# Expert results weighted per slot and added in DRAM by accumulating scatters onto the layer's input plus half the attention stream

## The reference, cut to what matters

```python
x = x + 0.5 * ffn(layernorm(x))        # f = 0
x = x + rwkv(layernorm(x))
x = x + 0.5 * ffn(layernorm(x))        # f = 1

def ffn(h0):                           # 16 heads, 4 key/value heads, 8 experts, 2 per token
    h = h0 + attention(rmsnorm(h0))
    return h + moe(rmsnorm(h))

def moe(xt):
    topv, topi = top_k(xt @ gate_w, 2)
    w = one_hot(topi) weighted with softmax(topv)
    for e in range(8):
        out += w[:, e:e + 1] * ((silu(xt @ w1[e]) * (xt @ w3[e])) @ w2[e])
```

## Time and profile before

| | us |
|---|---|
| median of 3 runs | 1247.35 |
| lowest, highest | 1242.57, 1247.72 |
| profiled execution | 1246.85 |
| its span (first to last instruction) | 1245.0 |
| PE busy in the span | 1167.7 (94%) |
| DVE busy | 939.9 (75%) |
| ACT busy | 798.2 (64%) |
| POOL busy | 567.9 (46%) |

### The profile page before, as it was taken

How to read it: one execution, slowest core, us unless ns; L and a number is a source line. 1 busy time by engine, 2 the same in 40 slices (tenths; PEclk the granted TensorE clock), 3 DMA queues, 4 the chain that set the end, 5 groups by cost and what they waited for, 6 DMA issues and landing times.

```text
span 1245.0 us, 18860 instructions
## 1 busy us (share of the span) xinstructions
PE 1167.7 (94%) x6572; PEld 977.5 (79%) x6572; DVE 939.9 (75%) x1990; ACT 798.2 (64%) x1573; POOL 567.9 (46%) x421
## 2 busy tenths in 40 slices
PE   4899999999999899996998899999999999899994
PEld 3788888888888578883687688888888888758883
DVE  6777887887897777767787777787787798677773
ACT  5666666666666467775565766676676666467773
POOL 3666666666640034430001495675685660025441
PEclk9999999999999999998999999999999999999997
DMA  4100100100013452252101000100100010751113
GB/s 138 39 1 1 39 1 1 39 1 1 2 51 136 152 175 66 65 136 85 56 1 42 31 1 1 29 11 1 35 4 2 1 52 1 254 189 52 52 52 123
DMA packets 48685, 65.93 MB, mean 53 GB/s; under 512 B 5840, under 2 KB 34384, under 8 KB 48464
## 3 DMA queue, kind: packets, MB, share of 16 engines
q1 hardware_dynamic: 42064, 50.56, 12.9%
q0 software_dynamic: 4416, 12.06, 3.2%
q10 hardware_dynamic: 2112, 2.10, 0.5%
HBM read 54.48 MB, written 10.22 MB: 52 GB/s over the span
## 4 chain that ended last, share of the span: by engine, by line
PE 44%; DVE 4%; ACT 2%; issue 1%; DMA 1%; POOL 1%; SPq 0%; DVEq 0%; ACTq 0%; POOLq 0%
PE ps L1631 11%; PE ps L1633 11%; PE ps L1632 11%; PE ps L1701 5%; PE ps L1783 3%; PE ps L1612 1%; PE ps L1771 1%; PE ps L1844 1%; DVE h L1217 1%; DMA mixT<-y_dram 0%; PE ps L1753 0%; ACT probs L812 0%; DVE ps L1195 0%; PE ps L1821 0%; POOL probs L684 0%
## 5 line engine op out<-in xcount | busy, mean ns | idle before, releaser
L812 ACT ACTIVATE probs<-ps,negmax 128x128 f32<-128x128 f32 (+7 forms) x256 | 189.7, 741 | 89.1 <-DVE negmax L1195 86.0
L818 ACT ACTIVATE probsT<-ps 128x512 fp32r<-128x512 f32 x288 | 170.3, 597 | 112.2 <-PE ps L1701 110.7
L1201 DVE TENSOR_TENSOR probsT<-ps,probsT 128x512 fp32r<-128x512 f32 x288 | 195.8, 685 | 46.4 <-ACT probsT L818 45.0
L1195 DVE CUSTOM_DVE_ANT_0 ps<-ps,causal 128x128 f32<-128x128 f32 (+7 forms) x256 | 193.3, 761 | 28.5 <-PE ps L1633 26.4
L688 POOL TENSOR_TENSOR crossed<-crossed,rope 128x512 f32<-128x512 f32 x70 | 90.4, 1291 | 193.2 <-ACT crossed L798 193.1
L1701 PE MATMUL ps<-square,probs 128*128 128x128 f32 x1152 | 171.3, 274 | 5.7 <-ACT probs L812 5.3
L1701 PEld LDWEIGHTS ps<-square,probs 128*128 128x128 f32 x1152 | 141.5, 141 | 35.1 <-issue 4.2
L735 POOL DMA_INDIRECT xs<-rows_dram,token_of x46 | 69.1, 1501 | 180.7 <-DVE token_of L1282 158.2
L1217 DVE SCALAR_TENSOR_TENSOR h<-ps,rowinv,h 128x256 f32<-128x256 f32 x256 | 123.3, 482 | 36.3 <-PE ps L1633 27.6
L1303 DVE TENSOR_TENSOR parts<-experts,parts 128x1024 fp32r<-128x1024 f32 x92 | 112.3, 1225 | 49.1 <-ACT parts L862 48.6
L1631 PE MATMUL ps<-keysT,queriesT 128*128 128x512 f32 (+4 forms) x384 | 141.8, 369 | 3.3 <-DVE straight L1171 1.4
(11 more groups left out here) (254 smaller groups left out, 2846.9 us busy)
## 6 DMA issues: line engine op xcount, KB each, us to landing
experts<-in_L_ffn_w_dram SPq DMA_DIRECT2D x48, 512.0 KB, 6.7
w_in<-in_L_ffn_wq_dram SPq DMA_DIRECT2D x8, 512.0 KB, 4.0
wo_in<-in_L_ffn_wo_dram SPq DMA_DIRECT2D x8, 512.0 KB, 6.0
rows_dram<-probs ACTq DMA_DIRECT2D x4, 512.0 KB, 3.0
probs<-y_dram SPq DMA_DIRECT2D x8, 256.0 KB, 4.5
mixT<-y_dram SPq DMA_DIRECT2D x8, 256.0 KB, 5.5
probs<-in_L_attn_x_dram SPq DMA_DIRECT2D x2, 512.0 KB, 4.5
w_in<-in_L_ffn_wk_dram SPq DMA_DIRECT2D x8, 128.0 KB, 4.8
```

Of the source, the lines that this page charges most:

```text
L812: act.activation(probs[:, i % 2, k, 0:w], ps[:, 2 * slot_n:2 * slot_n + 2, :].rearrange("p b n -> p (b n)")[:, at:at + w], ACT.Exp, bias=n ...
L818: act.activation(probsT[:, m % 3, 0, :], ps[:, 4 + m % 2, :], ACT.Copy).then_inc(S["probsT_high"], 1)
L1195: dve.tensor_tensor_reduce(out=row, in0=row, in1=causal[:, T - w:T], scale=-1.0, scalar=LARGEST, op0=ALU.add, op1=ALU.min, accum_out=negma ...
L1201: dve.tensor_tensor(probsT[:, m % 3, 1, :], ps[:, 4 + m % 2, :], probsT[:, m % 3, 0, :].bitcast(F32), ALU.subtract).then_inc(S["probsT_low ...
```

## The change

The two choices of a token are no longer written to separate rows and combined on chip. Each expert row is multiplied by its weight on the way out of PSUM (ACT's scale operand, `slot_wts`, one weight per slot and tile), and POOL's scatter adds it in DRAM to the token's row of a sum (`sums[f]`: `sum_dram` in f = 0, the output tensor itself in f = 1). That sum starts as the layer's input (copied from the input in DRAM at the start, or stored from x at the RWKV layer's end), and 0.5 h is added to it by eight accumulating scatters of 128 rows (`add_half`). Unused slots add to 128 spare rows behind the sum.

[...] ACT makes the halves before its first split. The weights per slot come from 32 more products of `in_place` with `wt_marks`, the weights in two float16 parts; `in_place` becomes a plain 0/1 matrix for that, and `marks` carries the choice numbers. After the loop SP loads the finished sum in f = 0 and nothing in f = 1, where the kernel ends when the last scatter has landed. `weigh`, `combine` and `base` are gone. In the first tiles the order changes: `up` of tile 1 comes before the transposes of tile 0's hid on PE, xs of tile 1 is turned in the middle of `up` of tile 0, and owner is made before the split of expert 0. Three of the SPINS are smaller.

```diff
-SPINS = (11, 18, 20, 54, 40, 12)
+SPINS = (9, 18, 15, 34, 40, 12)
...
-    small[:, C_SPARE:C_PLACE] = 1 + TOPK * T + P * np.arange(NS) + r[:, None]
+    small[:, C_SPARE:C_PLACE] = T + r[:, None]
...
+    sums = [sum_dram, out.rearrange("a t d -> (a t) d")]
...
 sync: attention_weights(0)
+                    given = a["L0_attn_x"].rearrange("a t d -> (a t) d")
+                    sp.dma_start(sum_dram[0:T], given).then_inc(S["base_in"], 16)
+                    for dst in sums:
+                        sp.dma_start(dst[T:T + P], given[0:P]).then_inc(S["spare_in"], 16)
...
-                    sp.dma_start(xsave, x).then_inc(S["saved"], 16)
+                    sp.dma_start(sum_tiles[1], x).then_inc(S["saved"], 16)
...
-                for n in range(NT // 2):
-                    pair = slice(2 * n, 2 * n + 2)
-                    sp.dma_start(x[:, pair, :], y_choices[0, :, pair, :]).then_inc(pair_in[n], 16)
-                    sp.dma_start(second[:, pair, :], y_choices[1, :, pair, :]).then_inc(pair_in[n], 16)
             attention_weights(0)
             moe(0)
+            sp.wait_ge(S["added"], 16 * NS)
+            for n in range(NT // 2):
+                pair = slice(2 * n, 2 * n + 2)
+                sp.dma_start(x[:, pair, :], sum_tiles[0][:, pair, :]).then_inc(pair_in[n], 16)
             attention_weights(1)
+            moe(1)
             sp.wait_ge(S["saved"], 16)
-            moe(1)
-            for n in range(NT // 2):
-                sp.wait_ge(S["x_sum"], NT + 2 * n + 2)
-                sp.dma_start(out_dram[:, 2 * n:2 * n + 2, :], x[:, 2 * n:2 * n + 2, :]).then_inc(S["stored"], 16)
-            sp.wait_ge(S["stored"], 16 * (NT // 2))
+            sp.wait_ge(S["halves_in"], 16 * NT * 2)
+            sp.wait_ge(S["added"], 16 * NS * 2)
...
 gpsimd
+            def add_half(f, t):
+
+                pool.wait_ge(S["halved"], NT * f + t + 1)
+                pool.indirect_dma_start(
+                    out=sums[f], out_offset=bass.IndirectOffsetOnAxis(ap=token_ids[:, t:t + 1], axis=0),
+                    in_=half_h[:, t, :], in_offset=None, compute_op=ALU.add).then_inc(S["halves_in"], 16)
+
             def scatter(f, tau):
 
-                par = tau % 2
                 pool.wait_ge(S["ys_ready"], NS * f + tau + 1)
+                if NS * f + tau:
+                    pool.wait_ge(S["added"], 16 * (NS * f + tau))
                 pool.indirect_dma_start(
-                    out=y_dram, out_offset=bass.IndirectOffsetOnAxis(ap=row_of[:, tau:tau + 1], axis=0),
-                    in_=ys[:, par, :], in_offset=None).then_inc(added[par], 16)
+                    out=sums[f], out_offset=bass.IndirectOffsetOnAxis(ap=row_of[:, tau:tau + 1], axis=0),
+                    in_=ys[:, tau % 2, :], in_offset=None, compute_op=ALU.add).then_inc(S["added"], 16)
...
+                for t in range(NT // 2):
+                    add_half(f, t)
                 pool.wait_ge(S["rows_stored"], 32 * (f + 1))
                 pool.wait_ge(S["token_ready"], f + 1)
                 gather(f, 0)
                 gather(f, 1)
+                for t in range(NT // 2, NT):
+                    add_half(f, t)
...
+                    if tau == 1:
+                        pool.wait_ge(S["halves_in"], 16 * NT * (f + 1))
                     if tau:
                         scatter(f, tau - 1)
...
 scalar: take_ys
                 if tau >= 2:
-                    act.wait_ge(added[par], 16 * (PAR[par] * f + tau // 2))
-                act.activation(ys[:, par, :], ps[:, 7, 0:D], ACT.Copy).then_inc(S["ys_ready"], 1)
+                    act.wait_ge(S["added"], 16 * (NS * f + tau - 1))
+                else:
+                    act.wait_ge(S["slot_wts_ready"], f + 1)
+                act.activation(ys[:, par, :], ps[:, 7, 0:D], ACT.Copy, scale=slot_wts[:, tau:tau + 1]).then_inc(S["ys_ready"], 1)
...
+                for t in range(NT):
+                    act.activation(half_h[:, t, :], h[:, t, :], ACT.Copy, scale=0.5).then_inc(S["halved"], 1)
...
 vector: route
-                dve.tensor_tensor(marks[:], small[:, C_TILE:C_TILE + NS]...
+                dve.tensor_tensor(in_tile[:], small[:, C_TILE:C_TILE + NS]...
...
+                dve.tensor_tensor(marks[:], in_tile[:], small[:, C_CHOICE:C_SPARE].rearrange("p (c o) -> p c o", o=1)
+                                  .broadcast_to([P, CHOICES, NS]), ALU.mult).then_inc(S["marked"], 1)
                 for n in range(CHOICES):
-                    dve.tensor_scalar(in_place[:, n, :], place16[:], placef[:, n:n + 1], small[:, C_CHOICE + n:C_CHOICE + n + 1],
-                                      ALU.is_equal, ALU.mult).then_inc(S["marked"], 1)
+                    dve.tensor_scalar(in_place[:, n, :], place16[:], placef[:, n:n + 1], None, ALU.is_equal
+                                      ).then_inc(S["marked"], 1)
...
+                for part in range(2):
+                    dve.tensor_tensor(wt_marks[:, part], in_tile[:], wts16[:, part, :].rearrange("p (c o) -> p c o", o=1)
+                                      .broadcast_to([P, CHOICES, NS]), ALU.mult).then_inc(S["parts_ready"], 1)
+
+            def slot_weights(f):
+
+                dve.wait_ge(S["slot_wts_ps"], f + 1)
+                dve.tensor_scalar(slot_wts[:, 0:NS], ps[:, 7, 256:256 + NS], 1.0 / WT, None, ALU.mult).then_inc(S["slot_wts_ready"], 1)
...
 tensor
+            def slot_weights(f):
+
+                for part in range(2):
+                    pe.wait_ge(S["parts_ready"], 2 * f + part + 1)
+                    for n in range(CHOICES):
+                        last = pe.matmul(ps[:, 7, 256:256 + NS], in_place[:, n, :], wt_marks[:, part, n, :],
+                                         start=(part + n == 0), stop=(part == 1 and n == CHOICES - 1))
+                last.then_inc(S["slot_wts_ps"], 1)
...
                 turn_xs(f, 0)
+                slot_weights(f)
                 up(f, 0)
-                turn_xs(f, 1)
+                up(f, 1)
```

136 lines of the change are left out of this document (60 added, 76 removed).

## The result

The changed kernel takes 1255.93 us (median of 4 runs, 1254.77 to 1256.49) against 1245.07 us before in the same series. The ratio is 1.0084, 95% interval 1.0066 to 1.0101: slower by 0.84%, where 1231.7 us was forecast. The profiled execution took 1256.27 us (span 1254.5), 9.4 more than before's 1246.85.

What follows compares the result with a forecast made beforehand. TensorE was taken to set the pace in the tile loops and to starve behind them. From the profiled 1246.85 us, terms of -11.9 (end), -4.2 (behind f = 0) and +1.0 (starts) gave 1231.7 us; range 1223 to 1243.

Steps and rivals of the forecast that it cites:

- Part 4: Start of each mixture: added DVE work and POOL's accumulates against savings, -1.2 to +4 us a start, taken as +1.0 for two.
- Rival C: Mixture starts: third gather 2.5 us late, first by 1, TensorE's clock falling; +3.5 to +4 us a start, 1238 us; chance 0.15.
- Part 1: End of f = 1: loads and combines gone, program ends when chained scatter 22 lands at 1233.05, not 1245.0; -11.9 us.
- L: Time from a scatter's issue to its landing; accumulating ones taken as 3.7 us in f = 1, 4.2 in f = 0.
- Rival D: Accumulation nearly free, landing in 2.5 us or so after a scatter's issue: 1224.3 us; chance 0.12.
- Part 2: Behind f = 0: four DVE combines gone (-6.7 us) against the chained scatter landings (+2.5); -4.2 us.
- Part 3: Tile loop: POOL's 4.3 us cycle fits the 5.15 us tile, TensorE stays the bound; 0 us.
- rival B: Tile loop: chained scatters become the bound, landing in 5.47 us, every tile pays; 1255.4 us, slower; chance 0.13.

Runs made afterwards that it cites:

- e1: Changed kernel without the eight accumulating scatters of 0.5 h and the waits on them (0.5 h missing in the result): 1237.8 us.
- e9: Changed kernel with 32 filler matmuls instead of 15 ahead of the first transposes of xs: 1256.44 us.
- e10: Changed kernel, 0.5 h added to reloaded x by GpSimd (five tiles behind VectorE's small routing steps, three behind gathers), SyncE storing it; 19 fillers: 1244.33 us.
- e13: Changed kernel, 0.5 h added to reloaded x by GpSimd in two four-tile blocks behind the third and fourth gathers, stored by SyncE; 19 fillers: 1242.13 us.
- e5: Kernel before the change with one more gather of 128 rows, unused, late on GpSimd's queue: 1252.52 us.
- e3: Changed kernel with every accumulating scatter made a plain one, rows overwritten instead of added to: 1237.01 us.
- e7: Changed kernel with the loads of Wr, Wv, Wcr and Wo behind the loads of the sum in f = 0: 1264.57 us.
- e15: Changed kernel, halves added by two direct accumulating DMAs, seven tiles before the routing, then the eighth; 19 fillers: 1236.15 us.
- e12: Changed kernel, the eight half scatters replaced by one direct accumulating DMA ahead of the first gather; 19 fillers: 1242.49 us.
- e14: Changed kernel, the eight half scatters replaced by one direct accumulating DMA behind the third tile's gather; 19 fillers: 1246.55 us.
- e8: Changed kernel in which GpSimd waits for the last expert scatter's landing before its program ends: 1258.18 us.

## Why the prediction was wrong

**Part 4, the starts: forecast +1.0, measured +19.1; this is the step that failed.** The forecast had four accumulates over at 1101.0, 12.9 us behind the table load; they took until 15.7. Its pitch of 1.62 us was that of two plain gathers; an accumulating scatter is issued in 1.55, with its gap 1.87, and three of the sixteen, those begun 0.03 to 0.31 us behind the start of a split on VectorE, in 2.33 to 2.61. The first also left 7.2 us behind the table load, 0.8 later than the sum had it. The second four were to end 22.5 us behind the table load; they ended at 27.4. The third gather then landed in 5.75 us, not 3. The 1.58 of the loop's gather, read as a warning, was the better number. Why that landing took 5.75 us stays open; the landings of the halves issued before it took 5.3 (median), but e1's third gather, with no halves, took 6.7.

Rival C named the place and the wait, at half the size in f = 0 and a third in f = 1: +3.5 to 4 a start against 7.8 and 11.3. Its clock did fall, to 0.50 from 1113.4 to 1116.0, but e9 shows that this adds nothing of its own beside the late third gather. The other terms of Part 4 held: e1 has them all and starts 0.4 and 1.3 us longer than before, which is inside the -1.2 to +1.3 that the forecast's ranges give without POOL's stall.

VectorE and GpSimd slowed each other in e10 and e13; why, no run shows. VectorE's in_place steps took 5.24 us beside GpSimd's additions (e10) against 2.69 (e1), its two splits 3.51 against 2.36 (e13), and in e13 four additions on GpSimd took 4.82 beside those splits against 3.88 for the first four. The issues of the halves were long beside the splits, as told above, but 1.55 to 1.69 us beside in_place. No row of the kernel before has a half to show this. Known in advance, it would have moved weight to C, whose 1238 us was still too low.

**Part 1, the end: forecast -11.9, measured -6.6** (-8.3 + 1.6). The landing was right: L = 3.84 (1246.06 to 1249.9) against 3.7. The 0.1 us for POOL's wake-up stands in no row; scatter 22 left 0.76 us behind the landing of 21 (1245.30). "SP ends there" was wrong: POOL's DRAIN holds the end for 4.6 us more. It stood in the trace of before, 8.79 us from 1228.1, hidden by the combination; e5 shows that it alone can set the end. Rival D falls: no run shows an accumulating landing at its L of 2.5 or so; only the plain ones come near it, 2.41 before and 2.39 in e3.

**Part 2, behind f = 0: forecast -4.2, measured -2.2.** The stretch with the combines was -7.1 (forecast -6.7). The chained landing was +4.9, forecast +2.5; without the weight loads beside it (e7) it is +2.6. The step left out four loads of 256 KB that SyncE issues at 562.55 to 563.98.

**Part 3, the loop: 0, right.** Scatters are 5.15 us apart and TensorE is full (ACT's copy with the scale takes 0.47 us, 0.38 before, which costs nothing there), so rival B did not happen in the loop, though the time came out near its 1255.4: the right number for another reason. Its mechanism stands only at the end of f = 0, where a landing beside weight loads exceeds a tile's 5.15 us (5.8 for the scatter of 562.80, for which that of 569.36 waits 5.01 us).

Sum of errors: 18.1 + 5.3 + 2.0 - 0.8 for the attention parts = 24.6 us.

## What to carry to other kernels

An instruction added to a queue is paid by what stands behind it, at its own issue time there: count the issues up to the next one that somebody waits for, and take no other instruction's pitch. Bulk additions in DRAM belong into one DMA, so early that it has landed before the next gather on that queue (e15 against e12 and e14). A strict chain of transfers is paid where a landing gets longer than a step of the loop (5.8 us against 5.15 at the end of f = 0), so look at its last links beside other loads. When a change takes away the work at a program's end, look for what that work had hidden, the closing DRAIN of GpSimd's queue first (8.4 us here).

## What the runs showed of the hardware

- An accumulating scatter of 128 rows of 1 KB: 1.54 to 1.61 us to issue in f = 1 of the changed kernel, 3.8 to land (median); a plain one 0.97 to 0.99 to issue and 2.41 to land at the end of the kernel before, 0.96 and 2.39 at the end of e3.
- Begun 0.03 to 0.31 us behind the start of VectorE's split (parts<-experts,parts, 128x1024 f32) the issue of a half took 2.33 to 2.61 us in the changed kernel, 1.56 when begun 0.76 ahead of one (440.91), and 1.55 to 1.69 beside the in_place steps.
- One direct accumulating DMA of 1 MB: 1.7 to 1.8 us to issue, 9.5 to 9.7 to land (e12), 15.5 to 16.7 beside expert loads (e14); a gather issued 3.4 us behind it lands in 6.6 us in e12, in 2.8 in e1.
- GpSimd's closing DRAIN ends 7.8 to 8.9 us behind the issue of GpSimd's last DMA in all but two runs, 10.1 in e3, and 10.5 in e8, where the landing was waited for first and the DRAIN itself took 6.3. Why it is that long in e3 stays open.
- The 16 one-scalar in_place steps take 2.69 us, 0.17 each (e1), against 3.66 with two scalars; beside issues on GpSimd they take 2.90 (changed kernel, accumulating) and 2.93 (e3, plain).
